# Finishing the second expert layer's rows per slot tile and scattering them straight into the output

## The reference

```python
x = x + _L1_ffn_ref(_layernorm(x)[None], gate_w, gate_b, w1, b1, w2, b2)[0]

# _L1_ffn_ref, T = 6250 rows, D = 256, F = 1024, E = 8 experts, C = ceil(1.25 * T / E) = 977 places each
probs = softmax(x @ gate_w + gate_b); idx = argmax(probs); prb = probs[idx]
pos = rank of the row among the rows of its expert;  kept = pos < C
hmid = relu(buf[e] @ w1[e] + b1[e]);  ybuf = hmid @ w2[e] + b2[e]
y_tok = ybuf[idx, min(pos, C - 1)] * (prb * kept)
y = nan_to_num(y_tok, nan=0.0, posinf=10000.0, neginf=-10000.0)
```

## Time and profile before

| | |
|---|---|
| time, 3 runs | 5373.17, 5381.75 (median), 5383.99 us |
| profiled execution: span | 5371.9 us; its time around the span is not given |
| PE busy | 4172.9 us (78%) |
| DVE busy | 3413.4 us (64%) |
| POOL busy | 2167.4 us (40%) |
| ACT busy | 1663.0 us (31%) |
| second layer's combining stage, first load to the end | 5283.6 to 5371.9 us |

### The profile page before, as it was taken

The page is one execution under the profiler, slowest core; times in us unless marked ns, Lnnn a source line. Parts: engine busy times, 40 slices in busy tenths (PEclk is TensorE's granted clock), DMA queues, the critical chain, the costliest instruction groups (busy, mean ns, idle before and its releaser), DMA issues. The chain is left out here.

```text
span 5371.9 us, 86748 instructions
## 1 busy us (share of the span) xinstructions
PE 4172.9 (78%) x27330; PEld 3017.8 (56%) x27331; DVE 3413.4 (64%) x7289; ACT 1663.0 (31%) x2903; POOL 2167.4 (40%) x2194
## 2 busy tenths in 40 slices
PE   3477777777777777746999945999999999769992
PEld 2355555555555555534888833666656666458872
DVE  6466666666666666687555577888888888640115
ACT  1233333333333333321222264333333333121121
POOL 1477777777777777700666600000000000202220
PEclk9678777777777887756999966999999999759996
DMA  4766666666666666651566543444444444323333
GB/s 122 189 168 170 167 165 170 170 162 170 170 165 167 170 169 163 158 207 68 193 200 199 183 139 84 81 85 89 81 81 88 87 81 85 88 86 121 100 118 103
DMA packets 946866, 733.83 MB, mean 137 GB/s; under 512 B 703102, under 2 KB 832054, under 8 KB 944599
## 3 DMA queue, kind: packets, MB, share of 16 engines
q1 hardware_dynamic: 835851, 433.62, 31.3%
q0 software_dynamic: 104144, 289.95, 20.0%
q10 hardware_dynamic: 6652, 7.32, 0.4%
HBM read 483.39 MB, written 92.34 MB: 107 GB/s over the span
## 5 line engine op out<-in xcount | busy, mean ns | idle before, releaser
L1288 POOL DMA_INDIRECT gat_rows<-h_rows,gat_sources x1664 | 1577.0, 948 | 509.2 <-issue 485.5
L1526 PE MATMUL gat_sum_ps<-gat_rows,gat_onehot 128*128 128x265 f32 x3328 | 1167.6, 510 | 3.2 <-DVE gat_rows L1418 2.4
L1526 PEld LDWEIGHTS gat_sum_ps<-gat_rows,gat_onehot 128*128 128x128 f32 x3328 | 792.9, 250 | 190.4 <-issue 5.7
L2055 ACT CAST gnn_z<-build_ps 128x392 bf16<-128x392 f32 x992 | 473.4, 486 | 847.7 <-PE build_ps L2070 842.3
L1997 DVE TENSOR_TENSOR onehot_low<-dense_codes,dense_iota_bf 128x2048 bf16<-128x2048 bf16 x496 | 604.0, 1218 | 2.6 <-PE build_ps L2070 2.6
L2080 PE MATMUL back_ps<-zb_pieces,gnn_z 128*128 128x384 bf16 x3038 | 567.1, 327 | 0.0
L2102 PE MATMUL front_ps<-x_res_wide,front_rows 128*128 128x448 bf16 x2604 | 562.5, 353 | 0.0
L1976 POOL DMA_INDIRECT front_rows<-zf_piece_rows,vrow_nodes x62 | 64.8, 1046 | 1231.2 <-PE front_ps L2102 1221.0
L1418 DVE TENSOR_TENSOR gat_rows<-gat_rows,gat_numerators_ps 128x1024 f32<-128x1024 f32 x416 | 502.0, 1207 | 0.0
L2471 PE MATMUL moe_hidden_ps<-moe_rows_T,moe_w 128*128 128x256 f32 (+1 forms) x1408 | 459.9, 483 | 2.7 <-DVE moe_rows_T L2512 0.8
L2070 PEld LDWEIGHTS build_ps<-onehot_high,onehot_low 128*128 128x128 bf16 x7936 | 339.4, 98 | 204.6 <-issue 38.5
(11 more groups left out here) (366 smaller groups left out, 5160.4 us busy)
## 6 DMA issues: line engine op xcount, KB each, us to landing
moe_w<-in_L_ffn_W SPq DMA_DIRECT2D x112, 512.0 KB
gat_targets<-gat_step_targets SPq DMA_DIRECT2D x104, 512.0 KB
moe_w<-in_L_ffn_w SPq DMA_DIRECT2D x32, 1024.0 KB
gat_rows<-h_rows,gat_sources POOLq DMA_INDIRECT x1664
moe_rows_out<-moe_slot_zeros SPq DMA_DIRECT2D x36, 512.0 KB
gat_flags<-gat_tile_flags SPq DMA_DIRECT2D x104, 128.0 KB
normal_rows<-moe_xn_all SPq DMA_DIRECT2D x14, 896.0 KB
mid_taken<-moe_rows_out SPq DMA_DIRECT2D x14, 896.0 KB, 7.3
```

What stands on the lines that cost most here:

```text
L1288: pool.indirect_dma_start(out=g[:, b, t, :], out_offset=None, in_=T.h[:, :], in_offset=bass.IndirectOffsetOnAxis(ap=idx[:, b, t:t + 1], ax ...
L1526: last = pe.matmul(po[:, s % BANKS, 0:W], o[:, b, s * SUB + t, :], g[:, b, s * SUB + t, :], start=t == 0, stop=t == SUB - 1)
L2055: nc.scalar.copy(AT[:, k % 2, :, CHUNK * c:CHUNK * (c + 1)], pb[:, c % 2, 0:CHUNK * NT].rearrange("p (u h) -> p h u", u=CHUNK)).then_inc(a ...
```

## The change

In the second expert layer only (`direct` is set):

- `copies`: at the start of `project_nodes`, SP issues 7 DMAs that store `x_res` beside the normalised rows (the new DRAM tensor `T.pair` has 2 KB rows: normalised, residual) and 8 that prefill the output with `x_res`.
- `route` also makes the weight of each slot: POOL builds a third one-hot per row tile, scaled by the row's weight, and PE's product has 128 columns instead of 64.
- `experts` gathers 2 KB rows. After each bias add DVE runs `finish`: six more instructions on the slot tile, each after the one before where it needs it. POOL scatters the finished rows to the output; rows for the unused slots have targets beyond the output and are dropped by the bounds check. `take(t)` waits in addition for `finish` of all tiles of group t-2, since `finish` reads the residual half of the buffer that `take(t)` overwrites.
- `combine`, `T.y2` and its zero fill are gone.

In both layers:

- the wait for the stores of normalised rows moves from the end of `project_nodes` to SP in `route`.
- `put` waits tile by tile, not for all Q tiles.

```diff
 # project_nodes, SP
+            if keep is not None:
+                keep.copies(sp)
             if zeroed:
                 sp.wait_ge(zm, 1)
                 filled = zero_fill(sp, zeroed, zf, zs)
...
-                sp.wait_ge(xs, 16 * (S.NT // GROUP))
 # route
-        ot = k.sb(ctx, f"{tag}_onehot_tile", [P, RING, tiles])
+        ot = k.sb(ctx, f"{tag}_onehot_tile", [P, RING, parts, tiles])
-        pi = k.ps(ctx, f"{tag}_slot_ps", [P, tiles])
+        pi = k.ps(ctx, f"{tag}_slot_ps", [P, parts, tiles])
...
+            if slot_weight is not None:
+                c.link(dve.tensor_copy(slot_weight[:, :], pi[:, 1, :]))
...
+        @block.sync
+        def _(sp):
+            sp.wait_ge(stored, 16 * (NT // GROUP))
+        @block.gpsimd
+        def _(pool):
+            if slot_weight is not None:
+                pool.wait_ge(wr, 1)
+                for m in range(choices * NT):
+                    n, i = m // NT, m % NT
+                    if m >= RING:
+                        pool.wait_ge(ou, m - RING + 1)
+                    pool.tensor_scalar(ot[:, m % RING, 1, :], C.iota[:, 0:tiles], hi[:, n, i:i + 1], weight[:, n, i:i + 1],
+                                       ALU.is_equal, ALU.mult).then_inc(ow, 1)
 # route, PE
                 pe.wait_ge(oh, m + 1)
+                if slot_weight is not None:
+                    pe.wait_ge(ow, m + 1)
 # experts, POOL
             def take(t):
                 if t >= 2:
                     pool.wait_ge(tp, 2 * (t - 1))
+                    if direct:
+                        pool.wait_ge(yd, (t - 1) * Q)
...
             def put(t):
-                pool.wait_ge(yc, (t + 1) * Q)
                 for q in range(Q):
+                    pool.wait_ge(yd, t * Q + q + 1)
+                    at = bass.IndirectOffsetOnAxis(ap=dst_of[:, t * Q + q:t * Q + q + 1], axis=0)
+                    if direct:
+                        pool.indirect_dma_start(out=y[:, :], out_offset=at, in_=yo[:, t % 2, q, :], in_offset=None,
+                                                bounds_check=S.N - 1, oob_is_err=False).then_inc(ys[t % 2], 16)
...
+            if direct:
+                direct.rows_ready(pool)
             for t in range(groups + 2):
...
+                if direct and t == 2:
+                    direct.out_ready(pool)
                 if t >= 2:
                     put(t - 2)
 # experts, DVE
                     dve.tensor_tensor(yo[:, b, q, :], py[:, q % 2, 0:D], b2s[:, b, :], ALU.add).then_inc(yc, 1)
+                    if direct:
+                        finish(b, t, q)
+            def finish(b, t, q):
+                v = yo[:, b, q, :]
+                done = t * (GUARD * Q) + (q * GUARD + 1)
+                dve.wait_ge(yc, t * Q + (q + 1))
+                dve.tensor_scalar(v, v, direct.weight[:, bass.ds(t * Q + q, 1)], None, ALU.mult).then_inc(gs, 1)
+                dve.wait_ge(gs, done + 1)
+                dve.tensor_scalar(cl[:, :], v, 1e4, -1e4, ALU.min, ALU.max).then_inc(gs, 1)
+                dve.tensor_tensor(ok[:, 0, :], v, v, ALU.not_equal).then_inc(gs, 1)
+                dve.tensor_scalar(ok[:, 1, :], v, 0.0, 0.0, ALU.mult, ALU.not_equal).then_inc(gs, 1)
+                dve.wait_ge(gs, done + 4)
+                dve.nop(nofuse=True)
+                dve.copy_predicated(v, ok[:, 1, :], cl[:, :]).then_inc(gs, 1)
+                dve.wait_ge(gs, done + 5)
+                dve.nop(nofuse=True)
+                dve.copy_predicated(v, ok[:, 0, :], lim[:, :].to_broadcast([P, D])).then_inc(gs, 1)
+                dve.wait_ge(gs, done + 6)
+                dve.tensor_tensor(v, v, xr[:, b, q, D:2 * D], ALU.add).then_inc(yd, 1)
 # combine removed; new:
+class Direct:
+    def begin(self, ctx, tiles):
+        self.weight = self.k.sb(ctx, "slot_weights", [P, tiles])
+    def copies(self, sp):
+        S, T, x = self.S, self.T, self.x_res
+        full, tail = rows_of(self.out, S)
+        pair = T.pair.rearrange("(i p) d -> p i d", p=P)[:, :, S.D:2 * S.D]
+        for g in range(S.NT // GROUP):
+            a, b = g * GROUP, (g + 1) * GROUP
+            sp.dma_start(pair[:, a:b, :], x[:, a:b, :]).then_inc(self.rs, 16)
+        for g in range(S.NT // GROUP):
+            a, b = g * GROUP, min((g + 1) * GROUP, S.NT - 1)
+            sp.dma_start(full[:, a:b, :], x[:, a:b, :]).then_inc(self.os, 16)
+        sp.dma_start(tail, x[0:S.TAIL, S.NT - 1, :]).then_inc(self.os, 16)
+    def rows_ready(self, pool):
+        pool.wait_ge(self.rs, 16 * (self.S.NT // GROUP))
+    def out_ready(self, pool):
+        pool.wait_ge(self.os, 16 * (self.S.NT // GROUP + 1))
 # gnn_moe_kernel
-        T.y2 = k.dram("moe2_rows_out", [S.ROWS + S.G2 * TOK2, D])
+        T.pair = k.dram("normal_and_residual_rows", [S.ROWS, 2 * D])
-            [T.y1[0:2 * S.ROWS, :], T.y2[0:S.ROWS, :]])
+            [T.y1[0:2 * S.ROWS, :]])
-        combine(k, S, "moe2", 1, weight, T.y2, x_res, True, out)
```

More of the change, by code:

```diff
@@ L291, in project_nodes @@
     ev = k.sem(f"{tag}_product_copied")
-    xs = k.sem(f"{tag}_xn_stored") if xn_all is not None else None
+    xs = stored
     zm = k.sem(f"{tag}_slot_zeros_ready") if zeroed else None
@@ L2177, in _, with route @@
                 c.mark(pool.tensor_tensor(x, x, back, ALU.add))
-def route(k, S, C, tag, tok, logits, bias, choices, n_exp, capacity, src_of, dst_of, weight, gtab):
+def route(k, S, C, tag, tok, logits, bias, choices, n_exp, capacity, src_of, dst_of, weight, gtab, stored, slot_weight):
     nc = k.nc
@@ L2603 @@
 class Namespace:
     pass
-def store_rows(k, S, x_res, out):
-    nc = k.nc
-    st = k.sem("output_stored")
-    with ExitStack() as ctx:
-        block = ctx.enter_context(nc.Block())
-        @block.sync
-        def _(sp):
-            full, tail = rows_of(out, S)
-            sp.dma_start(full, x_res[:, 0:S.NT - 1, :]).then_inc(st, 16)
-            sp.dma_start(tail, x_res[0:S.TAIL, S.NT - 1, :]).then_inc(st, 16)
-            sp.wait_ge(st, 32)
 def gnn_moe_kernel(nc, ins, out):
@@ L2684, in gnn_moe_kernel, with moe @@
         k.recycle()
-        def moe(weight, tag, tok, rhs, bias, choices, X, capacity, affine, groups, F, func, y, w, tables, zeroed):
+        def moe(weight, tag, tok, rhs, bias, choices, X, capacity, affine, groups, F, func, y, w, tables, zeroed, direct=None):
             with ExitStack() as ctx:
+                stored = k.sem(f"{tag}_xn_stored")
+                xn_rows = T.xn
+                if direct:
+                    direct.begin(ctx, groups * tok // P)
+                    xn_rows = T.pair
                 src_of = k.sb(ctx, f"{tag}_slot_source", [P, groups * tok // P], I32)
```

114 lines of the change are left out of this document (36 added, 78 removed).

## The result

The changed kernel takes 5291.23 us, the median of four runs (5283.09 to 5295.13), against 5381.84 us for the kernel before in the same comparison: a ratio of 0.9832, 95% interval 0.9818 to 0.9845. The forecast was 5289. The profiled execution took 5283.09 us, with a span of 5281.3 us, where the one of before had 5371.9: 90.6 us less. Ranges, medians and ratios leave out one later execution of the kernel before (5631.2 us) and one of the best version (6805.8 us), in which the granted clock was 0.75 and 0.55 of full speed against 0.85 and 0.86 in the others. That the total agrees to 2 us hides a term that was missed by 8.4 us (D): terms A and E were missed by 2.0 and 1.05 us in the same direction, and B, C, the tile-wise scatters and 5.0 us in stretches that the change doesn't touch went the other way.

A forecast was written before the change was run, and what follows sets the result against it. PE was taken to bound the expert loop, with an uncovered combining stage behind it. A -90.6, B -6.4, C +3.5, D +1, E 0 sum to -92.5: 5381.75 becomes 5289 us, range 5279 to 5318.

The forecast's parts named there:

- Term A: End of kernel: combining stage goes, leaving last bias add, finish, one scatter; -90.6 us, bounds -91.5 and -88.
- Term B: Block ends of both projections: moved store wait is hidden in route; -3.2 us per layer, -6.4 in all, bounds -7 and -4.
- Zero fill and prefill: Shorter first-layer zero fill buys nothing; second-layer stores of 12.8 MB are hidden with 50 us of cover; cost 0.
- Rival 4: Second layer: prefill delays the first gather; at 80 GB/s +38 us, time 5327; chance 2%.
- Term D: Slot loop: POOL's added instruction, taken as 0.2 to 0.3 us per tile, is hidden; +1 us, bounds 0 and +98.
- rival 2: Slot loop becomes POOL's: instruction of 0.6 to 0.9 us, POOL possibly held by DVE; +8 to +24 us, time 5305; chance 12%.
- Term C: Start of second expert loop: doubled gather rows delay the first transpose; +3.5 us, bounds 0 and +7.5.
- Term E: Steady second expert loop: gathers waiting for finish still land 2.3 us before PE wants them; 0, bounds 0 and +50.
- Rival 1: Steady second expert loop: gathers come late, 1.8 us in 14 groups; +25 us, time 5314; chance 20%.
- Tile-wise scatters in the first layer: First expert layer: first scatter issued one tile earlier beside PE-bound work; 0, bounds -5 and +5 us.

The follow-up runs named there:

- best version: Changed kernel with slot weight one-hots on ScalarE and spread source rows for empty slots; 5280.83 us against 5288.18 for the changed kernel in the same rounds.
- run 2: Changed kernel with scatters waiting for all tiles of their group again, both layers; first expert loop's end 1.62 us longer, tail 12.77 us against 9.17.
- run 1: Changed kernel with the wait for the normalised rows' stores back at each projection's end; gaps 4.52 and 4.57 us instead of 0.88 and 0.82.
- run 10: Changed kernel with the longer first-layer zero fill back, output prefill and its wait removed; first-layer gap 0.88 us, second projection differs by 0.02 us.
- run 4: Changed kernel with eight buffers instead of four in the slot loop, POOL still making weight one-hots; slot loop 30.80 us against 31.09.
- run 9: Changed kernel with second-layer empty slots reading spread source rows instead of row 0; third turn 28.61 us against 29.86, expert loop 464.56 us.
- run 5: Changed kernel with the guard's first predicated copy done twice; second expert loop 471.90 us, +6.75, and tail 9.76 us.
- run 7: Changed kernel with the first predicated copy done twice and separate gathers for residual rows, only these waiting for the guard; loop 465.47 us, tail 15.64 us.
- run 8: Changed kernel without the guard's clamp, two compares and two predicated copies; expert loop 465.41 us, tail 6.89 us, 2.28 us shorter.

## Why the prediction was right, step by step

- **Term A (-90.6, measured -88.6): mechanism right, one part too small.** The guard's chain from the bias add's start to the finished tile was put at 3.3 us and is 3.55 in the last tile (5272.11 to 5275.66). In run 2, where no scatter is issued beside the last tile, it is 3.29: beside the scatter the finite test takes 0.52 us there instead of 0.29. By the trace the plain forms of 256 elements take 0.41 to 0.42, as in the sum; scaling takes 0.35 and not 0.41. The Trainium skill ("VectorE: DVE Perf Modes", section on the TRN2 errata) states 151 fixed cycles for a plain two-input add in float32, 0.42 us at this length, and the trace agrees. Carried over to the predicated copy with a scalar this would be 0.42 too, an estimate that the page doesn't make; it takes 0.50. From DVE's end to the scatter's start I had 0.29, from the earlier trace rows; it is 0.81. In the trace POOL's wait now sits on a register move of its own, which ends at 5275.73, and the DMA starts 0.73 us later; before, the DMA itself carried the wait. And from the scatter's start to the end I had 3.5 us, from no row; it is 4.8: the scatter has landed 2.3 us after its start, and then POOL's drain takes 2.02. That drain was in the trace of before, behind the same loop (at 5281.3, 2.01 us), and I had not looked for it. These 1.3 us make up most of the error of 2 us.
- **Term B (-6.4, measured -7.4): right**, shown by run 1. The error of 1.0 is the block boundary, put at 1.37 us and measured at 0.88 and 0.82.
- **Zero fill and prefill (0, measured 0): right**, shown by run 10. Rival 4 did not occur.
- **Term D (+1, measured +9.4): the size of one instruction was wrong, and rival 2 is what happened.** I took 0.2 to 0.3 us for POOL's instruction from the iota's 0.18, the row nearest in size but of another kind, and set the 0.17 beside it, which is the large row scaled by length and so leaves no fixed part at all. It takes 0.57 to 0.78, and it starts every 0.61 us. The rival had 0.6 to 0.9 us and +8 to +24, time 5305. Its price is borne out at the low end. Its reason, that DVE holds POOL, is the smaller part: with DVE at rest the instruction still starts only every 0.553 us (run 4), which alone gives 49 x (0.553 - 0.43) = +6 us by the prediction's own working. By which way DVE adds the rest was not tested.
- **Term C (+3.5, measured +1.4): too large.** The doubled rows cost this stretch 1.4 us in the profile and 0.9 to 1.4 in the others. The fourth gather is issued as early as before, since a gather of 2 KB rows takes POOL 0.95 us like one of 1 KB, and the DMA engines have the weights to move beside it either way.
- **Term E (0, measured +1.05): right in nearly all turns, for a smaller margin than stated.** The fourth gather's start was put 7.4 us after the last bias add's start and is 8.0 (5186.12 to 5194.14), from the longer chain and the 0.5 us more at POOL's wait. The landing was put at 3.4 us and takes up to 3.7 in most turns and 4.8 in some. Against 2.3 us, most turns have at least 1.85 to spare, some less than 1, and the last 0.25. The +1.05 is one turn, and its cause, a group of empty slots reading one row, was not among the steps. That reading one row is what makes it late is shown by run 9, with run 10 as the case that it doesn't explain. Rival 1 had the right handover but not the right size; run 5 shows what it would have cost: 6.75 us for gathers up to 1.85 us later, in six turns and not 14.
- **Tile-wise scatters in the first layer (0, measured -1.6): wrong**, because I argued from the steady loop where the last group counts.
- **The sum.** The terms predicted -92.5 and measure -85.7. By them alone the time would be 5381.75 - 85.7 = 5296 us. The remaining -5.0 us lie in stretches that the change doesn't touch; their cause stays open. The forecast came within 2 us of the median by luck in good part: term D was wrong by 8.4 us, and that drift and the smaller misses hid it.

## What to carry to other kernels

Before a step is given to an idle engine because it is small, look for a row of the same kind of instruction on that engine, not of the same size on another kind: here an instruction of about 0.6 us on GpSimd turned a hidden half into the bound of its loop, and ScalarE did the same work for 1 us, two small instructions ahead of the loop included. What is hidden in the steady state of a loop is bare behind its last step, so follow the last tile to the very end of the program, drain included. And a total that comes out right is no proof of its terms: compare stretch by stretch, and hold the stretches that nothing touched against their own variation.

## What the runs showed of the hardware that was not expected

- **GpSimd's small instruction.** A compare and multiply of 128x64 elements with two scalars per partition takes 0.57 us with VectorE at rest (run 4) and 0.57 to 0.78 beside it; on VectorE the same form takes 0.31, and ScalarE's scaled copy of that size 0.35.
- **GpSimd's drain at the end of a block with indirect DMAs.** 2.0 us after 128 of them in the second expert loop (2.01 before, 2.02 after), 7.9 after 192 in run 7, 5.1 after 286 in the first expert loop, 22 after 1652 in an earlier block, and 7.7 to 8.1 after only 60 in the graph convolution. Where it follows an expert loop it lies on the path: nothing else runs in the block by then. It does not grow evenly with the count, and its rule stays open.
- **Reads of one row.** A burst of 512 gathers of row 0 has packets of 267 ns in the median (up to 370 in other executions), where other bursts have 159, and moves 160 GB/s in a stretch where the spread one moves 414.
- **VectorE beside a DMA issue of GpSimd.** The finite test of 256 elements takes 0.52 us while the scatter before it is issued, and 0.29 in run 2, where none is.
- **A pause in GpSimd's issues.** In the second expert loop the second gather of the last group starts 2.04 us after the first has ended, where it is 0.30 otherwise, in every run with 2 KB gathers; before and in run 7 it doesn't occur.
- **An earlier start doesn't mean an earlier landing.** In run 8 the gathers start 2.05 us earlier in the turn, while the next group's weights still come in, and the third turn waits as long as before.
